# Graph layer on one core: cycles of eight gathered groups and one picked group, and a fill before each gather

## The reference

```
h   = maximum(layernorm(x), 0)                      # 12500 x 48
z   = concat([h[dst], h[src], edge_attr]) @ W1 + b1  # 400000 x 128
msg = relu(z) @ W2 + b2                              # 400000 x 48
out = x + segment_sum(msg, dst)                      # 12500 x 48
```

## Time and profile before

| | |
|---|---|
| median of 3 runs | 3659.81 us (3658.93 to 3660.19) |
| the profiled execution | 3658.51 us, span 3656.7 us |
| instructions in the span | 87220 |
| granted TensorE clock, mean | 0.886 of 2.4 GHz |

### The profile page before, as it was taken

How to read it: one execution, slowest core, us unless ns; L and a number is a source line. 1 busy time by engine, 2 the same in 40 slices (tenths; PEclk the granted TensorE clock), 3 DMA queues, 4 the chain that set the end, 5 groups by cost and what they waited for, 6 DMA issues and landing times.

```text
span 3656.7 us, 87220 instructions
## 1 busy us (share of the span) xinstructions
PE 3025.8 (83%) x18452; PEld 2737.9 (75%) x18452; DVE 2276.9 (62%) x6092; ACT 1575.4 (43%) x6025; POOL 2755.9 (75%) x2916
## 2 busy tenths in 40 slices
PE   6688889888888888888887788888788888888787
PEld 6687878787778877777877677777677877777677
DVE  8666666666666666666656566666666666656653
ACT  6344444444444444444444444444444444444432
POOL 7777777777777777777777777777777777777776
PEclk9988898888988799899889998989998889898975
DMA  9533343443333333333333333333333333333334
GB/s 278 113 102 104 101 106 100 105 104 102 105 101 102 99 102 97 102 98 102 95 103 97 101 96 101 98 103 99 98 102 97 102 95 103 96 104 96 102 94 102
DMA packets 310442, 384.87 MB, mean 105 GB/s; under 512 B 98901, under 2 KB 250262, under 8 KB 309239
## 3 DMA queue, kind: packets, MB, share of 16 engines
q0 software_dynamic: 92864, 187.75, 20.3%
q1 hardware_dynamic: 217238, 195.30, 19.0%
q10 hardware_dynamic: 208, 0.57, 0.1%
HBM read 366.25 MB, written 16.97 MB: 105 GB/s over the span
## 4 chain that ended last, share of the span: by engine, by line
PE 38%; DMA 23%; issue 13%; DVE 10%; POOL 9%; DVEq 4%; SPq 2%; ACT 1%; POOLq 0%; ACTq 0%
DMA gath<-b_table,idx 23%; PE ps L1299 13%; PE ps L1327 9%; POOL gath L558 8%; PE ps L1308 8%; DVE gath L1020 5%; DVEq L1023 2%; PE ps L1347 1%; DVE work L1069 1%; PE ps L1315 1%; PE ps L1316 1%; PE ps L1354 1%; PE ps L1273 1%; PE ps L1336 1%; DVE nodes L1036 1%
## 5 line engine op out<-in xcount | busy, mean ns | idle before, releaser
L558 POOL DMA_INDIRECT gath<-b_table,idx x2838 | 2678.4, 944 | 866.7 <-issue 770.7
L1299 PEld LDWEIGHTS ps<-rhs,lhs 96*128 96x128 f32 x5676 | 858.5, 219 | 810.8 <-issue 706.4
L1299 PE MATMUL ps<-rhs,lhs 96*128 96x128 f32 x5676 | 960.5, 313 | 598.8 <-DVE gath L1020 575.8
L1327 PE MATMUL ps<-h_tab,p_hot 128*128 128x480 f32 (+1 forms) x4104 | 1165.5, 415 | 0.0
L679 ACT ACTIVATE gath<-gath 128x384 f32<-128x384 f32 x946 | 494.5, 523 | 1519.1 <-DVE gath L1020 1518.4
L1020 DVE TENSOR_TENSOR gath<-ps,gath 128x384 f32<-128x384 f32 x946 | 524.3, 554 | 727.7 <-DMA gath<-b_table,idx 698.7
L1308 PE MATMUL ps<-onehot,gath 128*128 128x48 f32 x5676 | 833.1, 288 | 11.3 <-ACT gath L679 11.3
L1308 PEld LDWEIGHTS ps<-onehot,gath 128*128 128x128 f32 x5676 | 821.7, 216 | 17.7 <-ACT gath L679 11.8
L1327 PEld LDWEIGHTS ps<-h_tab,p_hot 128*128 128x128 f32 x4104 | 782.0, 211 | 41.9
L698 ACT ACTIVATE work<-ps,work 128x80 f32<-128x80 f32 x2508 | 625.1, 403 | 7.1 <-PE ps L1308 6.2
L1008 DVE TENSOR_SCALAR_CACHE_REDUCE lhs<-nodes 48x384 f32<-48x384 f32 x946 | 577.1, 610 | 44.7 <-issue 14.1
(11 more groups left out here) (127 smaller groups left out, 1284.9 us busy)
## 6 DMA issues: line engine op xcount, KB each, us to landing
nodes<-dst_row SPq DMA_DIRECT2D x946, 72.0 KB
lhs<-in_edge_t SPq DMA_DIRECT2D x946, 48.0 KB
gath<-b_table,idx POOLq DMA_INDIRECT x2838
rhs<-a_table SPq DMA_DIRECT2D x946, 24.0 KB
work<-key_row SPq DMA_DIRECT2D x57, 256.0 KB
nodes<-dst_row SPq DMA_DIRECT2D x73, 96.0 KB
work<-in_edge_t SPq DMA_DIRECT2D x146, 32.0 KB
b_table<-nodes SPq DMA_DIRECT2D x7, 512.0 KB, 3.7
```

What stands on the lines that cost most here:

```text
L558: pool.indirect_dma_start(gath[:, u, t, :], None, b_table, bass.IndirectOffsetOnAxis(ap=idx[:, v, t:t + 1], axis=0)).then_inc(gathered[u], 16)
L1299: mm = nc.tensor.matmul(ps_z[:, k % 2, t * P:(t + 1) * P], lhs[:, u, t * P:(t + 1) * P], rhs[:, u, :], start=True, stop=True)
L1327: nc.tensor.matmul(ps_run[:, q, 0:m * words].rearrange("p (j w) -> p j w", j=m), p_hot[:, t % 2, i, :], h_tab[:, first:first + BLOCKS * (m ...
```

## The change

Two things change together.

1. The cycle has PERIOD = 8 steps in place of 16. A picked group then comes with every eight gathered groups. A run of nine matmuls is no longer cut in two: `run_p(r, c, it)` does a whole run at step j = r, waits for its key compare, and counts it in a new semaphore `p_run_done`, for which `pick` and `key_hot` wait. There are 108 cycles and 12 extra steps: 4 + 108 x 8 + 12 = 880 steps, 107 picked and 16 early groups. The work of a picked or early group's tail is placed anew over the eight steps of a cycle and the start of the next; the masks are made in two halves; the biases of the two kinds of tail have a buffer each.
2. GpSimd fills one word per partition of a new tile `spacer` in front of each gather, and a wait keeps a fill from overtaking that of the same place eight steps ago.

```
-PERIOD = 16
+PERIOD = 8
-RUN_BLOCKS = (5, 4)
-CYCLES = 58
-EXTRA = 14
+CYCLES = 108
+EXTRA = 12
-PAD_TILES = 5
+PAD_TILES = 7
...
+        spacer = sb("spacer", [P, IDX_SLOTS, STEP_TILES[0]])
...
                 if k >= SLOTS:
                     pool.wait_ge(summed, s - SLOTS + 1)
+                    pool.wait_ge(spaced, STEP_TILES[0] * (it * PERIOD + max(k - IDX_SLOTS + 1, 1)))
                 pool.sem_inc(waited)
                 for t in range(step_tiles(k)):
+                    nc.gpsimd.memset(spacer[:, v, t:t + 1], 0.0).then_inc(spaced, 1)
                     pool.indirect_dma_start(
...
-            def run_p(r, h, c, it):
+            def run_p(r, c, it):
                 n, t, q = c + it, r // 2, r % 2
-                if h == 0 and (r >= 2 or c):
+                if q == 0:
+                    pe.wait_ge(p_hot_ready, n * TILES + t + 1)
+                if r >= 2 or c:
                     pe.wait_ge(p_picked, n * runs + r - 1)
-                for i in range(RUN_BLOCKS[0] * h, RUN_BLOCKS[0] + RUN_BLOCKS[1] * h):
+                for i in range(BLOCKS):
...
+                mm.then_inc(p_run_done, 1)
...
             def pick(r, c, it):
                 n, t, q = c + it, r // 2, r % 2
-                act.wait_ge(summed, step_summed(c, 2 * r + 2, it))
-                act.wait_ge(p_mask_ready, n + 1)
+                act.wait_ge(p_run_done, n * runs + r + 1)
+                act.wait_ge(p_mask_ready, 2 * n + t // 2 + 1)
...
                     if not final:
-                        run_p(j // 2, j % 2, c, it)
+                        run_p(j, c, it)
```

More of the change, by code:

```diff
@@ L90, in gnn @@
     assert n_tiles == ALL_TILES and cycles > EARLY + 5
-    assert BLOCKS * PARTS >= node_tiles and RUN_PARTS[0] * words <= BANK and 2 * runs == PERIOD
-    assert sum(RUN_BLOCKS) == BLOCKS
-    assert PERIOD == 4 * SLOTS and LEAD == SLOTS and early_tiles == EARLY_A + EARLY_B + EARLY_C
+    assert BLOCKS * PARTS >= node_tiles and RUN_PARTS[0] * words <= BANK and runs == PERIOD
+    assert PERIOD == 2 * SLOTS and LEAD == SLOTS and early_tiles == EARLY_A + EARLY_B + EARLY_C
     assert rounds * gen_cols * gen_k == n_nodes and front_piece * pieces == front
@@ L727, in cycle @@
                         take_idx(k + IDX_AHEAD, it)
-                    if j == 1 and not first:
+                    if j == 0 and not first:
                         pick(runs - 1, c - 1, it)
-                    if j % 2 and 1 < j < PERIOD and not final:
-                        pick((j - 3) // 2, c, it)
+                    if 0 < j < PERIOD and not final:
+                        pick(j - 1, c, it)
                     if (k - 3) % FOLD == FOLD - 1:
                         copy_sums(k - 3, it)
-                    if j == 10 and not first:
+                    if j == 2 and c >= 2 or j == 6 and 0 < c <= EARLY or j == PERIOD + 2:
                         copy_sums_tail(k - 3, it)
[L736 to L743, removed]
+                    if j == 1 and 0 < c <= EARLY:
+                        keep_tail_h(place_e(c - 1, it), step_summed(c, 0, it))
+                    if j == 3 and 0 < c <= EARLY:
+                        rectify_tail(step_summed(c, 2, it), 0)
+                    if j == 5 and not first:
+                        keep_tail_h(place_p(c - 1, it), step_summed(c, 4, it))
+                    if j == 7 and not first:
+                        rectify_tail(step_summed(c, 6, it), 1)
                     if first and j == 5:
@@ L747, in cycle @@
                                              ).then_inc(early_std, 1)
-                    if c == 1 and j == 13:
+                    if c == 1 and j == 6:
                         act.wait_ge(early_ready, 4)
-                    if j == 13 and c < EARLY:
+                    if j == 6 and c < EARLY:
                         keep_early(c, it)
-                    if j == 8 and not first:
-                        rectify_tail(step_summed(c, 7, it))
             keep_words(3)
@@ L1043, in key_hot @@
                 if t >= 2 or c:
-                    dve.wait_ge(summed, step_summed(c, 4 * t - 4, it))
+                    dve.wait_ge(p_run_done, n * runs + 2 * (t - 1))
                 else:
@@ L1125, in cycle @@
                         add_z(k - 3, it)
-                    if j == 4 and not first:
+                    if j == 0 and not first:
+                        sum_picked(2, c - 1, it)
+                    if j == 2 and not first:
                         sum_picked(3, c - 1, it)
                         unpack_words(c - 1, it)
-                    if j == 5 and not first:
-                        dst_hot_t_tail(p_group(c - 1, it), place_p(c - 1, it), step_summed(c, 1, it) if c <= EARLY else step_summed(c - 1, 7, it))
@@ L1131, in cycle @@
[L1131 to L1136, removed]
+                    if j in (4, 6) and not final:
+                        sum_picked((j - 4) // 2, c, it)
+                    make_hot(k, it)
@@ L1137, in cycle @@
                     if j == 6 and not first:
-                        dst_hot_tail(p_tile(c - 1, it), step_summed(c, 3, it) if c <= EARLY else step_summed(c - 1, 9, it))
+                        dst_hot_tail(p_tile(c - 1, it), step_summed(c, 4, it) if c <= EARLY else step_summed(c, 0, it))
+                    if j in (1, 3, 5) and not final:
+                        key_hot((j + 1) // 2, c, it)
                     if j == PERIOD - 1 and more:
                         key_hot(0, c + 1, it)
-                    make_hot(k, it)
@@ L1142, in cycle @@
-                    make_hot_t(k, it)
-                    ends_e = 0 < c <= EARLY
+                        part_masks(0, c + 1, it)
+                    if j == 2 and not final:
+                        part_masks(1, c, it)
+                    ends_e = 1 < c <= EARLY + 1
                     if k % FOLD == 0 and k >= 2 * FOLD:
@@ L1149, in cycle @@
                         after = None
-                        if not first and j == 13:
+                        if j == 1 and ends_e:
+                            after = place_e(c - 2, it)
+                        if j == 5 and c >= 2:
+                            after = place_p(c - 2, it)
+                        if j == PERIOD + 5:
                             after = place_p(c - 1, it)
-                        if ends_e and j == 9:
-                            after = place_e(c - 1, it)
                         add_out(k - 6, it, after)
-                    if j == 12 and not first:
-                        add_out_tail(p_group(c - 1, it), step_summed(c, 11, it), it, k - 7)
[L1157 to L1162, removed]
+                    if j == 0 and ends_e:
+                        add_out_tail(c - 2 + it, step_summed(c - 1, 7, it), it, k - 7)
+                    if j == 4 and c >= 2:
+                        add_out_tail(p_group(c - 2, it), step_summed(c, 3, it), it, k - 7)
+                    if j == PERIOD + 4:
+                        add_out_tail(p_group(c - 1, it), step_summed(c, 11, it), it, k - 7)
                     if first and j == 4:
@@ L1206, in _ @@
                 add_z(k - 3, 0)
-            add_out(fetched - 5, 0)
-            add_out(fetched - 3, 0)
-            add_out(fetched - 1, 0)
+            for k in range(fetched // FOLD * FOLD - 7 if fetched % FOLD == 0 else fetched - 5, fetched, 2):
+                add_out(k, 0)
             dve.wait_ge(flag_ready, 1)
@@ L1374, in cycle @@
                         fold(k - FOLD, it)
[L1375 removed]
+                    if j == 0 and c >= 2:
+                        make_sums_tail(place_p(c - 2, it))
+                    if j == PERIOD:
+                        make_sums_tail(place_p(c - 1, it))
+                    if j == 0 and ends_e:
+                        turn_e(c - 1, it)
+                    if j == 2 and ends_e:
+                        make_z_tail(place_e(c - 1, it))
+                    if j == 4 and ends_e:
                         make_sums_tail(place_e(c - 1, it))
[L1377 removed]
+                    if j == 4 and not first:
                         turn_p(c - 1, it)
[L1379 to L1381 removed]
+                    if j == 6 and not first:
                         make_z_tail(place_p(c - 1, it))
[L1383 to L1388, removed]
+                    if j == 3 and c >= 2:
+                        fold_tail(place_p(c - 2, it), 1)
+                    if j == PERIOD + 3:
+                        fold_tail(place_p(c - 1, it), 1)
                     if j == 7 and ends_e:
[L1390 removed]
+                        fold_tail(place_e(c - 1, it), 0)
                     make_sums(k - 3, it)
                     if not final:
[L1393 removed]
+                        run_p(j, c, it)
                     if final and j == 2:
```

65 lines of the change are left out of this document (37 added, 28 removed).

## The result

The changed kernel takes 3447.55 us (median of 4 runs, 3446.26 to 3449.33); the kernel before took 3660.0 beside it. The ratio is 0.942, with a 95% interval of 0.9408 to 0.9432. The forecast was 3562, so the direction is right and the gain of 212 us is more than twice the 98 that were forecast.

What follows compares the result with a forecast made beforehand. GpSimd's gathers, 1.2492 us apart, were taken as the bound. Span 3656.7 - 247 (fewer gathers) + 132 (fills) + 18 (early cycles) = 3559, so 3562 us as median; range 3440 to 3730.

Steps and rivals of the forecast that it cites:

- What bound the kernel before: Main loop on GpSimd: the number of gathers times 1.2492 us sets the span; other engines follow that pace.
- Fewer gathers, -247 us: GpSimd's gathers go from 2838 to 2640 at unchanged spacing, so the span falls to 3409.4 us.
- The end: Program after the last gather: stays 13.2 us, with a microsecond at most added because the last fold holds four groups.
- The fill, +132 us: GpSimd, one-word fill before each of 2640 gathers: each adds 0.05 us, as POOL has no slack.
- the rival built on it: Fill before each gather is free or helps; PE becomes the bound, 3450 to 3496 us; chance 0.24.
- rival C: Fill before each gather makes the 0.30 us be paid afresh: 4201 or 4439 us; chance 0.11.
- More picking on PE, hidden at 3.71: PE, nine picking matmuls per step: 3.71 us at full clock, hidden by 5% under POOL's 3.898.
- The early cycles, +18 us: PE in cycles 1 to 16: early tails make 4.04 us a step, over POOL's 3.898, on 128 steps.
- VectorE, 3.47 to 3.76: VectorE's work per step in us, including idle before output additions; at the lower end hidden under 3.898, but lumpy.
- The clock: TensorE's granted clock: taken as full, since PE would idle only some 0.2 us a step.
- ScalarE: ScalarE's picks go from 2508 to 4708, +548 us on 1575: 60% of the span, off the path.
- SP's key loads at nothing: 256 KB key loads every 8 steps on SP: cost taken 0; without cover up to 1 us a cycle, +107.

## Why the prediction was off

**What bound the kernel before** was read right: GpSimd, one gather every 1.2492 us. PE, the busiest engine with 83%, was no bound, and its stretches at half clock cost nothing, since the spacing of the gathers stayed even through them.

**Fewer gathers, -247 us:** right. 801 gathers in 1000 us stand at the old pace in the late cycles, and the run without fills takes the same time. The end, taken to grow by "a microsecond at most", grew by 3.7.

**The fill, +132 us: this is the step that failed.** The term was mis-sized: 0.05 each was forecast, 0.000 measured (2838 of them and 0.6 us, inside the interval). The rule behind the number was wrong, not only the number. The prediction took the price from start to start at the beginning of the program, 0.05, and charged it on top of the 1.249, because nothing on that engine seemed free ("each adds its price m whole: POOL has no slack at all"). But the 0.30 in front of each gather is not idle that every new instruction pushes back: one fill, or two at 0.029 each, pass through it. Even the price from start to start was too high; between gathers it is 0.029. The bound "nothing, if the fill fits inside the 0.30" was stated, and the rival built on it got 0.24. The iota behind the last gather was the row to weigh: it starts at the gather's end, so the engine is free to start other work in that gap. The prediction used it only to say that leaving a gather costs nothing, and against rival C.

By the dispatch that the Trainium skill gives for a GpSimd instruction (GPSIMD Engine Reference, section Instruction dispatch) the sum would have been 53 to 211 us, the prediction's estimate from that page. The measured 0.029 per further fill lies at the low end of that estimate, 0.02 to 0.08 each. The same section says that completion does not hold back the next Pool instruction, and the trace agrees: fills of 0.116 us follow each other every 0.029. Neither tells that the first two are free.

**More picking on PE, hidden at 3.71:** right in kind, 0.05 too high (3.66 by the run with ten matmuls), since a run of nine takes 1.87 and not 1.94. **The early cycles, +18 us:** the size follows from the wrong fill price. Against 3.748 the prediction's own 4.04 gives 128 x 0.29 = 37; 35 were measured. Relieving PE gave back only 22 of them, because the engines behind it were close.

**VectorE, 3.47 to 3.76:** at least at its lower end, or a little high. The estimate from the doubled sum is 3.38, not measured by itself, and the term that shrank can be read: the idle time in front of line 1036 was taken as 0.22 to 0.51 a step and is 121.6 us over 880 steps, 0.14. **The clock:** 0.988 on the mean and full wherever PE is dense, as taken. **ScalarE:** 62% busy for 60% forecast, off the path. **SP's key loads at nothing:** the late cycles stand at 1.248 a gather, so they cost nothing there; in the early cycles they were not tried apart.

With the fill at nothing, the prediction's own terms give 3409.4 + 37 + 3 = 3449 for a median of 3447.55. In spans it is 3446.4 for 3447.5, with 2 us too many for PE and 3 too few for the program's two ends.

What is left open: why a gather begins 0.30 us after another one's end but 0.15 after the end of the last of four or eight fills, and which part of the 13 us that remain in the early cycles is VectorE's, the slots' or the key load's. No kernel here beats the changed one with the whole computation; without its fills it is equally fast and simpler.

## What to carry to other kernels

Find the engine whose spacing never varies; here that one was the bound, at 75% busy beside another at 83%. Then ask of each gap on that engine whether it is a wait or part of the next instruction, before an added instruction is charged on top: adding one, two, four and eight of them gives the size of the cover and the price behind it. Work traded from a bound engine to a slack one is worth its full price only until the second engine's pace is met, and the idle share of an engine overstates its room: VectorE was 18% idle, and 0.53 us more a step, 14%, already cost time. Doubling an instruction is a cheap way to find that out.

## What the runs showed of the hardware

A one-column fill between two indirect DMAs of GpSimd is 0.112 to 0.119 us long on the mean of a run. One or two cost 0.00 us; from four to eight each further one costs 0.029. The 128-row gather stays at 0.944 to 0.946 us in every kernel.

On one chip the kernel before took 4659 to 4720 us, and the changed kernel's relatives 4500 to 4583. There a new entry stands among the waits, on GpSimd's fills for instance (the kernel with two of them):

```profile
L560 POOL MEMSET spacer<- 128x1 f32 x5280 | 374.6, 113 | 900.1 <-remote 442.9 <-PE ps L1317 292.0 <-issue 129.1
```

442.9 of the 900.1 us idle in front of the fills are put down to "remote", an entry that the profiles of the other chips do not have; VectorE and ScalarE have such waits as well. The gathers' own length was the same. The DMA engines moved 84 to 85 GB/s on the mean in place of 107 to 112, but these are the same 384 MB over a longer span and say nothing of the cause. What held the program up there is not shown.
